# Ring sizes in the deformable convolution: sampled tiles get five places for two, gathered tiles three for four

## What is computed

```python
x = x + _L0_conv_ref(_gn(x), ...)   # mixture of 8 experts on 2x2 patches, top 2
x = x + _L1_conv_ref(_gn(x), ...)   # deformable 3x3 convolution, batch norm, relu
x = x + _L2_conv_ref(_gn(x), ...)   # state-space layer: 16-tap filter, gelu, gated unit, layer norm
x = x + _L3_conv_ref(_gn(x), ...)   # 7x7 depthwise convolution, layer norm, two-layer MLP
```

```python
sampled = gather_corner(y0, x0, (1 - fy) * (1 - fx)) + gather_corner(y0, x0 + 1, (1 - fy) * fx) \
        + gather_corner(y0 + 1, x0, fy * (1 - fx)) + gather_corner(y0 + 1, x0 + 1, fy * fx)
sampled = sampled * mask[:, None]
out = jnp.einsum('bckhw,ock->bohw', sampled, w.reshape(CO, C, K2))
```

## Time and profile before

| what | us |
|---|---|
| median of the timed runs | 1748.08 |
| span of the profiled execution, first to last instruction | 2176.8 |
| busy: PE 1392.0, POOL 1190.0, DVE 953.2, ACT 526.5 | |
| first gather issued, last gather issued | 78.2, 1983.5 |
| 1152 gathers on POOL, busy | 1135.1 |
| POOL idle before gathers | 783.8 |

### The profile page before, as it was taken

The page is one execution under the profiler, slowest core; times in us unless marked ns, Lnnn a source line. Parts: engine busy times, 40 slices in busy tenths (PEclk is TensorE's granted clock), DMA queues, the critical chain, the costliest instruction groups (busy, mean ns, idle before and its releaser), DMA issues.

```text
span 2176.8 us, 13143 instructions
## 1 busy us (share of the span) xinstructions
PE 1392.0 (64%) x3780; PEld 595.6 (27%) x3780; DVE 953.2 (44%) x1562; ACT 526.5 (24%) x860; POOL 1190.0 (55%) x1393
## 2 busy tenths in 40 slices
PE   4647554496246877863366878855368874386976
PEld 3433212242112333322122333322123321132322
DVE  2424233354341333884532323875323328532564
ACT  1111111121112233211222333211213322132544
POOL 8655446357665555676565454676645566673000
PEclk9868766698567998986577889977678987687987
DMA  5212212132241111222141111222221112110100
GB/s 192 60 48 68 52 40 62 49 90 59 74 101 41 43 44 43 71 66 58 53 113 46 31 40 39 74 65 58 57 76 35 41 44 57 41 58 26 32 5 18
DMA packets 111591, 123.70 MB, mean 57 GB/s; under 512 B 50720, under 2 KB 88224, under 8 KB 111136
## 3 DMA queue, kind: packets, MB, share of 16 engines
q0 software_dynamic: 36864, 75.57, 12.5%
q1 hardware_dynamic: 73600, 43.82, 8.1%
q10 hardware_dynamic: 1056, 3.47, 0.4%
HBM read 99.79 MB, written 9.01 MB: 50 GB/s over the span
## 4 chain that ended last, share of the span: by engine, by line
PE 36%; another core or an unknown queue 27%; DVE 16%; issue 12%; ACT 7%; DMA 1%; SPq 1%; ACTq 0%; DVEq 0%
PE bank L1795 7%; PE bank L1808 7%; PE bank L1721 4%; DVE rb L1599 3%; PE bank L1717 3%; PE bank L1731 3%; DVE gt L1508 3%; PE bank L1752 2%; PE bank L1831 2%; PE bank L1783 2%; PE bank L1817 1%; DVE he L1406 1%; PE bank L1847 1%; PE bank L1772 1%
## 5 line engine op out<-in xcount | busy, mean ns | idle before, releaser
L1055 POOL DMA_INDIRECT gt<-corner_table,idx x1152 | 1135.1, 985 | 783.8 <-DVE sm L1516 392.4
L1795 PE MATMUL bank<-u,wk 128*128 128x512 f32 x512 | 256.7, 648 | 25.6 <-issue 9.6
L1808 PE MATMUL bank<-yg,wts 128*128 128x512 f32 x512 | 241.6, 615 | 46.9 <-ACT yg L1189 30.2
L1406 DVE SCALAR_TENSOR_TENSOR he<-he,bank 128x512 f32<-128x512 f32 (+1 forms) x144 | 90.2, 627 | 275.4 <-remote 88.9
L1721 PE MATMUL bank<-xg,w_sb 128*128 128x512 f32 (+1 forms) x288 | 149.3, 602 | 85.0 <-DVE xg L1397 61.9
L1772 PE MATMUL bank<-cst,sm 128*128 128x128 f32 x384 | 80.0, 322 | 187.0 <-ACT st L1173 79.7
L1540 DVE SCALAR_TENSOR_TENSOR tg<-tg,ae 128x512 f32<-128x512 f32 x64 | 44.5, 696 | 344.3 <-ACT ae L1201 270.9
L1731 PE MATMUL bank<-he,w_sb 128*128 128x512 f32 (+1 forms) x288 | 143.0, 580 | 54.6 <-DVE he L1406 30.9
L1508 DVE TENSOR_TENSOR gt<-gt,bank 128x1152 f32<-128x1152 f32 x128 | 172.5, 1347 | 0.9
L1599 DVE SCALAR_TENSOR_TENSOR rb<-xp,par,rb 128x1024 f32<-128x1024 f32 x124 | 155.1, 1291 | 0.0
L1125 ACT ACTIVATE he<-bank 128x512 f32<-128x512 f32 (+1 forms) x144 | 78.8, 549 | 294.3 <-PE bank L1717 166.7
(11 more groups left out here) (222 smaller groups left out, 1390.2 us busy)
## 6 DMA issues: line engine op xcount, KB each, us to landing
gt<-corner_table,idx POOLq DMA_INDIRECT x1152
tb<-gate_of_token SPq DMA_DIRECT2D x32, 256.0 KB
sqb<-gate_of_token SPq DMA_DIRECT2D x24, 256.0 KB
u<-sqb SPq DMA_DIRECT2D x48, 128.0 KB
corner_table<-tb SPq DMA_DIRECT2D x36, 128.0 KB, 2.7
w_sb<-w ACTq DMA_DIRECT2D x2, 1024.0 KB, 6.7
sqb<-gate_of_token SPq DMA_DIRECT2D x16, 128.0 KB
u<-xg SPq DMA_DIRECT2D x16, 128.0 KB
```

The lines of the kernel that those rows point to most:

```text
L1055: pool.indirect_dma_start(gt[:, t % GRING, k].rearrange("p a c -> p (a c)"), None, corners, bass.IndirectOffsetOnAxis(ap=idx[s % 2][:, j, ...
L1406: stt(out=he[:, u % 2, 0:w], in0=he[:, u % 2, 0:w], scalar=1.0, in1=psum[b][:, 0:w], op0=ALU.add, op1=ALU.mult).then_inc(free[b], 1)
L1795: op = mm(psum[b][:, :], wk[:, t, d], u4[:, g, at:at + HALF], start=t == 0, stop=t == JJ - 1 and n > 0)
L1808: op = mm(psum[B2.bank(*name)][:, :], w_glu[:, k, col + d * P:col + (d + 1) * P], yg[:, c % 2, k], start=k == 0, stop=k == NB2 - 1)
```

## The change

Two ring sizes. `GRING`, the places for gathered tiles in gt, goes from 4 to 3. The places for sampled tiles in sm, so far written as 2, become `SRING` = 5. Since 3 and 5 don't divide the 32 tiles of a step, the place of a tile is now reckoned over all steps, by `nth_tile`. The waits follow: gather of tile t on L1516 of t - 3, L1516 of tile t on PE's turn of t - 5. One place of gt is 9 x 4 x 32 x 4 = 4608 bytes a partition, three places of sm are 3 x 384 x 4 = 4608.

```diff
-GRING = 4
+GRING = 3
+SRING = 5
...
+def nth_tile(s, t):
+
+    return s * NT * GI + t
...
-        sm = sb("sm", [P, 2, 3 * P])
+        sm = sb("sm", [P, SRING, 3 * P])
...
                     pool.wait_ge(S["smp_ready"], FROM + s * NT * GI + t - GRING + 1)
+                i = nth_tile(s, t) % GRING
                 for k in range(KK):
                     pool.indirect_dma_start(
-                        gt[:, t % GRING, k].rearrange("p a c -> p (a c)"), None, corners,
+                        gt[:, i, k].rearrange("p a c -> p (a c)"), None, corners,
                         bass.IndirectOffsetOnAxis(ap=idx[s % 2][:, j, g * KK + k:g * KK + k + 1], axis=0),
-                    ).then_inc(gathered[t % GRING], 16)
+                    ).then_inc(gathered[i], 16)
...
-                i = t % GRING
-                dve.wait_ge(gathered[i], (s * (NT * GI // GRING) + t // GRING + 1) * 16 * KK)
+                i = nth_tile(s, t) % GRING
+                dve.wait_ge(gathered[i], (nth_tile(s, t) // GRING + 1) * 16 * KK)
...
-                if t >= 2:
-                    B1.filled(dve, "sampled", s, t - 2)
+                if t >= SRING:
+                    B1.filled(dve, "sampled", s, t - SRING)
                 elif s:
-                    B1.filled(dve, "sampled", s - 1, NT * GI + t - 2)
-                tt(sm[:, t % 2, 0:KK * C].rearrange("p (k c) -> p k c", k=KK), gt[:, i, :, 0], gt[:, i, :, 1],
+                    B1.filled(dve, "sampled", s - 1, NT * GI + t - SRING)
+                tt(sm[:, nth_tile(s, t) % SRING, 0:KK * C].rearrange("p (k c) -> p k c", k=KK), gt[:, i, :, 0], gt[:, i, :, 1],
                    ALU.add).then_inc(S["smp_ready"], 1)
...
-                    op = pe.transpose(psum[3][:, k * P:(k + 1) * P], sm[:, t % 2, k * P:(k + 1) * P], ident)
+                    op = pe.transpose(psum[3][:, k * P:(k + 1) * P], sm[:, nth_tile(s, t) % SRING, k * P:(k + 1) * P], ident)
```

## The result

The kernel after takes 1775.68 us (median, 1773.06 to 1779.11) beside 1748.20 us for the kernel before: ratio 1.0162, interval 1.0145 to 1.0180. That is 27.5 us slower; 1770.5 was forecast, in a range of 1744 to 1793.

A forecast was written before the change was run, and what follows sets the result against it. It took POOL's row of gathers, from 78 us on, to bound the timed runs. 1748.08 us plus 22.4 for the smaller gt ring, 0 for sm and 0 for small things gave 1770.5, range 1744 to 1793.

The forecast's parts named there:

- The bridge: From profile to timed runs: start, gathers without waits and tail sum to 1751.0 us against 1748.08, so POOL hardly waits.
- the remote waits of the earlier trace: DVE let go over 29 us after PE's recorded work at tile 25, step 1; timed runs mostly lack such waits.
- The two kinds of stretch: Places 4 to 15 of steps 1 and 2: PE busiest, ring fills; places 16 to 24: POOL never rests, ring runs dry.
- The size: Smaller gt ring: tile 27 of steps 0 and 1 loses a whole tile each, 2 x 11.2 = 22.4 us; steps 2, 3 nothing.
- the bounds of 10.4 and 45: Smaller gt ring: 10.4 us from the trace's margins at tile 27, 45 us if all four steps lose a whole tile.
- The landing: Time for a gather's data to land, without a row; 2.7 us taken from 128 KB writes and subtracted from tile 27's margins.
- Five places of sm at 0: L1516 waiting for PE's turn of t-5, not t-2: no effect, bounds 0 and a gain of 25.6 us.
- Rival A: Nothing measurable: three places of gt hold enough gathers ahead, loss 0 to 3 us, 1748 to 1751 us; chance 25%.
- Rival B: Faster: five sm places free DVE from waiting for PE at L1516, POOL gathers sooner, 1732.9 us; chance 12%.
- Rival C: Slower by more: all four points, and others such as tiles 2 and 3, pay a tile each, 1793 us; chance 18%.
- What would show it: Profile after: POOL's L1516 waits above 392.4 us, or as many with a shorter longest; L1516's waits for PE (82.0) gone.
- The signs at tile 27: DVE or PE idle just before L1508 there, or at tiles 2 and 3, with POOL in that same tile's nine gathers.

The follow-up runs named there:

- the first experiment: The kernel before, profiled once more with no edit: ratio 1.0010 to the kernel before, profiled span 1744.0 us.
- e8_ring3_light_pe: Kernel after, with 64 matmuls of the gated unit left out on PE in steps 1 and 2: 1762.1 us, 1.0053 of the kernel before.
- e2_ring3_sm2: Kernel after, with sampled tiles back at two places, so only the ring of gathered tiles is cut to three: 1.0146 of the kernel before.
- e3_ring4_sm3: Kernel after, with four places for gathered tiles, three for sampled ones, and last-layer MLP weights kept once per image: 1.0005 of the kernel before.

## Why the prediction was right, and where it wasn't

- **The bridge** (POOL hardly waits in the timed runs): right. 6.3 us of waits in the profile of before with the timed runs' span. Its numbers were partly luck, as the first experiment shows. That the remote waits of the earlier trace rows are not in the timed runs was right too: PE's late release at tile 27 of step 1 has no counterpart in the profiles with spans near 1750.
- **The two kinds of stretch**: right. The ring fills in places 4 to 15 and after the router's chain, and runs dry by tile 27; light work on PE takes the waits of steps 1 and 2 away (`e8_ring3_light_pe`).
- **The size**: 22.4 us forecast, 27.5 measured, within the bounds of 10.4 and 45. The step that failed is where and how much each step pays. I took two dry points at a whole tile, 11.2 us, and two at nothing. What is paid is POOL's waiting while the ring is full, 11.7, 9.7, 6.8 and 0 us in the four steps. Step 1 pays 9.7 (2.4 by its margin in the lower bound, a whole tile in the forecast), and step 2, put at nothing for its 15.0, pays 6.8. Nor is it only that the margins came from a disturbed profile: in the second one tile 27 lies 5.9, 10.2, 10.2 and 1.6 us behind its last gather, and step 3 with the smallest pays nothing, because its three places are never full when POOL wants one. Two whole tiles came near because steps 0 and 1 pay nearly one each, and that was partly luck.
- **The landing**: 2.7 us was taken from other writes. DVE starts 1.5 us after the end of the last gather when it has waited for it. This moved only the lower bound.
- **Five places of sm at 0**: right in effect (1.0146 against 1.0162, intervals overlapping). The reason given was too strong: it said that DVE would not have waited for PE even at tile 27, and the profile of before has one such wait, 11.6 us at tile 27 of step 0. It costs nothing that the runs show: POOL goes on gathering during it.
- **Rival A** (three places are enough) is out: two places cost 4.3% here, three 1.6%, and only with five is no wait left. The Trainium skill's main page (Trainium Kernel Development and Optimization, Best Practices) says to double-buffer, so that DMA and compute overlap. Read as "two places are enough", that fails for gt by these numbers, and for sm, where two do as well as five, it holds.
- **Rival B** (faster, by freeing DVE from PE) is out: `e2_ring3_sm2` and `e3_ring4_sm3`. **Rival C** (each of four points a tile) is out in size for three places; with two its sum would fit, but not its places (2.4 us of 80.6 at tiles 2 and 3, none behind tile 27).
- **What would show it**: that POOL's waits would pass 392.4 us failed, since that number belonged to a disturbed execution. The signs at tile 27, and the end of L1516's waits for PE, came as described; with two places for sm, too, the wait was down to one of 4.2 us.

Open: how much of step 0's waits belongs to the router's chain and how much to PE's places; and why the gathers' time in sum moves by up to 10 us from run to run, longest with five places. The longest gathers stand beside DVE's taps, so that more of them falling there is possible, but no run separated that.

## What to carry to other kernels

A ring between a steady producer that is the bound and a consumer that works in bursts costs what the producer waits while the ring is full; where it later runs dry is only where one sees it, and it can run dry without having cost anything. Count that waiting for each size: here 80.6, 34.5, 6.3 and 0 us for two to five places. From two to four the time follows it nearly one for one; of the last 6.3 us only about 2 came back with nothing left out, because the gathers grew longer. Places for the product behind the consumer didn't replace places in front of it here. That the order fixed by hand, which holds DVE to the engines behind it, is the reason was argued in the prediction and not tested.

## What the runs showed of the hardware

- A gather of 128 rows of 512 bytes takes 0.94 us on POOL in the median plus 0.30 until the next, whatever the ring. Single ones take up to 2.04 us, and in the profile after the longest, at 729.39, lies beside a tap on DVE (L1606, 729.33 to 730.61); the 108 gathers with more than half of their time beside taps take 1.12 us in the mean, the others 0.97. Over tile 22 of step 1 nine of them took 14.2 us, in the quiet places 10.9. In sum the 1152 gathers took 1142.2 us with two places, 1137.6 to 1144.7 with three, 1138.4 to 1142.1 with four and 1147.8 and 1148.2 with five.
- One execution under the profiler was 25% longer than the timed runs (2176.8 us), with the clock granted at 0.801 of full in the mean and DVE held for PE's release up to 32.9 us; the others of this case, 12 profiles, lie within 8 us of their timed medians, at 0.85 to 0.87. A profile whose span doesn't fit the timed runs should be taken again before margins are read from it.
